# Every matrix product in plain fp32 instead of three split fp32r passes, with the expert weights resident in SBUF

## The reference

```python
# attention, per sequence of n = 256 tokens
xn = layernorm(x) * g_norm
q  = l2norm(xn @ Wq per head) * q_scale              # 16 heads of 64
kv = xn @ Wkv                                        # one key head and one value head of 64
k, v = with a null key and value put in front (one vector, cond_64[0] and cond_64[1])
sim  = 8 * q @ k.T + relative_position_bias          # the bias is a small 3-layer network of i - j
attn = softmax(causal(sim)); out = concat_heads(attn @ v)
x = x + layernorm(out @ Wout) * g_out                # 1024 -> 256
# mixture of experts, per token
scores = softmax((x @ wt.T + cond @ wg.T) / 2)       # 8 experts, the best 2, weights normalised
y_e = (leaky(x @ w_gate[e]) * (x @ w_up[e])) @ w_down[e]      # 256 -> 128 -> 256
x = x + weighted sum of the two y_e + a shared expert of width 256 (as two more blocks of 128)
```

## Time and profile before

| what | us |
|---|---|
| median of three executions (1060.23 to 1061.74) | 1060.24 |
| the profiled execution: its time, its span | 1064.17, 1062.40 |
| to the first transposes of round 0's queries (span's start to 42.89) | 42.89 |
| the rest of round 0, to the transposes of round 1's input | 72.28 |
| rounds 1 to 6, each to the same transposes of the next round | 124.94 to 125.90 |
| round 7 to its output projection | 124.16 |
| output projection of round 7 and its experts | 69.57 |

### The profile page before, as it was taken

One profiled execution on the slowest core, in us unless ns is written; L12 is line 12 of the kernel. 1 busy time (PEld: TensorE's weight loads), 2 busy tenths in 40 slices (PEclk: granted clock), 3 DMA queues, 4 the chain that ended last, 5 costly groups with the idle time before them and its releaser, 6 DMA issues.

```text
span 1062.4 us, 21427 instructions
## 1 busy us (share of the span) xinstructions
PE 1014.6 (96%) x6788; PEld 815.3 (77%) x6788; DVE 707.4 (67%) x2457; ACT 526.5 (50%) x1564; POOL 437.0 (41%) x422
## 2 busy tenths in 40 slices
PE   3887999999999999999999999999999999999998
PEld 2665877778777887778777787777877788777877
DVE  8789577665867558665676647676576755856543
ACT  3488346651565435663456614665246643565220
POOL 1634154441554333642535515454245534444212
PEclk9899999999999999999999999999999999999999
DMA  5316414112132013311132212311123211232043
GB/s 198 80 54 215 151 60 122 53 66 63 61 110 90 28 55 101 100 61 61 43 118 72 71 42 79 112 65 46 62 66 113 82 41 41 84 106 71 20 138 102
DMA packets 40996, 87.68 MB, mean 83 GB/s; under 512 B 4192, under 2 KB 19040, under 8 KB 40624
## 3 DMA queue, kind: packets, MB, share of 16 engines
q1 hardware_dynamic: 39920, 83.57, 24.5%
q10 hardware_dynamic: 960, 2.62, 0.7%
HBM read 76.57 MB, written 9.60 MB: 81 GB/s over the span
## 4 chain that ended last, share of the span: by engine, by line
PE 75%; DVE 10%; issue 5%; ACT 4%; DVEq 0%; POOL 0%; ACTq 0%
PE psY L1641 13%; PE psS L1511 6%; PE psO L1547 5%; PE psG L69 5%; PE psG L71 5%; PE psG L70 5%; PE psT L1522 5%; PE psS L71 3%; PE psS L70 3%; PE psS L69 3%; PE psS L1507 3%; PE psT L1529 2%; PE psO L1550 2%; PE psT L69 2%; PE psT L71 2%
## 5 line engine op out<-in xcount | busy, mean ns | idle before, releaser
L604 POOL TENSOR_TENSOR work<-work,rden 128x514 f32<-128x514 f32 x128 | 134.0, 1047 | 322.3 <-DVE rden L1137 321.6
L1641 PE MATMUL psY<-Wd,H 128*128 128x256 f32 x640 | 172.5, 399 | 0.0
L763 ACT ACTIVATE work<-work,low 128x257 f32<-128x257 f32 x256 | 128.5, 504 | 60.1 <-DVE low L1155 59.5
L69 PE MATMUL psG<-x1T_hi,Wgu 128*128 128x512 f32 (+1 forms) x292 | 134.8, 462 | 2.6 <-ACT leaky L807 1.9
L1641 PEld LDWEIGHTS psY<-Wd,H 128*128 128x128 f32 x640 | 112.4, 190 | 29.4 <-issue 14.4
L1155 DVE CUSTOM_DVE_ANT_0 work<-psS,bias,null_s 128x256 f32<-128x256 f32 x256 | 113.3, 480 | 28.4 <-PE psS L1511 25.9
L1251 DVE SCALAR_TENSOR_TENSOR leaky<-leaky 128x512 f32<-128x512 f32 x80 | 56.4, 704 | 101.5 <-ACT leaky L807 100.5
L71 PE MATMUL psG<-x1T_lo,Wgu 128*128 128x512 f32 (+1 forms) x292 | 114.9, 394 | 0.0
L70 PE MATMUL psG<-x1T_hi,Wgu 128*128 128x512 f32 (+1 forms) x292 | 114.4, 392 | 0.0
L593 POOL TENSOR_TENSOR rq<-qss,neghalf 128x16 f32<-128x16 f32 x32 | 97.5, 3048 | 36.3 <-DVE qss L1131 36.3
L1511 PE MATMUL psS<-KB,qT 64*128 64x256 f32 (+1 forms) x1024 | 105.7, 325 | 0.0
(11 more groups left out here) (259 smaller groups left out, 2306.7 us busy)
## 6 DMA issues: line engine op xcount, KB each, us to landing
Wgu<-wexp SPq DMA_DIRECT2D x80, 512.0 KB, 3.4
Wb<-wscr SPq DMA_DIRECT2D x64, 256.0 KB, 3.6
wexp<-Wgu SPq DMA_DIRECT2D x10, 512.0 KB, 2.9
xres<-in_x SPq DMA_DIRECT2D x8, 512.0 KB, 4.7
xin<-in_x SPq DMA_DIRECT2D x7, 512.0 KB, 4.2
out<-work SPq DMA_DIRECT2D x7, 512.0 KB, 2.9
H<-in_wgu SPq DMA_DIRECT2D x10, 256.0 KB, 3.9
bias<-bscr SPq DMA_DIRECT2D x4, 512.0 KB, 6.6
```

The lines of the kernel that those rows point to most:

```text
L69: te.matmul(dst, a_hi, b_hi, start=start, stop=False)
L604: pool.tensor_tensor(T1[sl][:, hs, :], T1[sl][:, hs, :], rden[sl][:, 1, hs].unsqueeze(2) .to_broadcast([P, 2, N + 1]), ALU.mult)
L763: act.activation(T1[sl][:, h, :], T1[sl][:, h, :], ACT.Exp, scale=-1.0, bias=low[sl][:, 1, h:h + 1], accum_out=den[sl][:, 1, h:h + 1])
L1641: mm = te.matmul(psY[:, t // 2, (t % 2) * D:(t % 2 + 1) * D], H[:, k % H_RING, t * P:(t + 1) * P], Wd[:, ORDER[k], :], start=(k == 0 and t ...
```

## The change

All parts go: every product takes plain fp32 operands and is one `te.matmul` where `products` issued three. `products`, the `lo` tiles, all subtractions and the waits on them are gone; `keys` moves 144 columns instead of 256; head outputs are a ScalarE copy alone; of `xnT` and `x1T` ScalarE copies one half and VectorE the other. The expert weights are loaded once, in round 0, into an SBUF tile that holds all ten blocks, and `wexp`, the ring and the reloads are gone. TensorE waits for all ten loads at the place quoted above.

```diff
-def products(te, dst, a, b, start, stop):
-    (a_hi, a_lo), (b_hi, b_lo) = a, b
-    te.matmul(dst, a_hi, b_hi, start=start, stop=False)
-    te.matmul(dst, a_lo, b_hi, start=False, stop=False)
-    return te.matmul(dst, a_hi, b_lo, start=False, stop=stop)
...
-        Wgu = sb("Wgu", [P, W_RING, 2, 2, KC, P], F32R)
+        Wgu = sb("Wgu", [P, BLOCKS, 2, KC, P])
...
             load_norm_x(1)
-            for e in range(BLOCKS + 2):
-                if e < BLOCKS:
-                    if e >= H_RING:
-                        sp.wait_ge(parts_done.sem, e - H_RING + 1)
-                    sp.dma_start(H[:, e % H_RING, :], wgu[e].rearrange("p w c m -> p (w c m)")) \
-                        .then_inc(wraw_in[e % H_RING].sem, 16)
-                if e >= 2:
-                    sp.wait_ge(parts_done.sem, e - 1)
-                    sp.dma_start(wexp.ap()[e - 2], Wgu[:, (e - 2) % W_RING].bitcast(F32)) \
-                        .then_inc(parts_out[(e - 2) % W_RING].sem, 16)
-            sp.wait_ge(pre_v.sem, V_WOUT)
+            for k in range(BLOCKS):
+                sp.dma_start(Wgu[:, k], wgu[ORDER[k]]).then_inc(ld_gu.sem, 16)
             sp.dma_start(xres[:], x_t[0]).then_inc(xres_in.sem, 16)
...
-                act.activation(oT[0][:, STEPS * (g % 2) + s, (g // 2) * N:(g // 2 + 1) * N], value_bank(n)[:, 0:N],
-                               ACT.Copy).then_inc(o_lead.sem, 1)
+                act.activation(oT[:, STEPS * (g % 2) + s, (g // 2) * N:(g // 2 + 1) * N], value_bank(n)[:, 0:N],
+                               ACT.Copy).then_inc(o_done.sem, 1)
...
-            def head_out(r, n):
-                g, s = n // STEPS, n % STEPS
-                need(dve, o_lead, r, n + 1)
-                cols = (slice(None), STEPS * (g % 2) + s, slice((g // 2) * N, (g // 2 + 1) * N))
-                dve.tensor_tensor(oT[1][cols], value_bank(n)[:, 0:N], oT[0][cols].bitcast(F32), ALU.subtract) \
-                    .then_inc(o_done.sem, 1)
...
+            def x1_turned(m):
+                need(dve, x1T_ps, m, 2)
+                dve.tensor_copy(x1T[:, 1, :], psO[:]).then_inc(x1T_v.sem, 1)
...
-                        mm = products(te, psT[:, t // 2, (t % 2) * 2 * P:(t % 2 + 1) * 2 * P],
-                                      [part[:, c, t * P:(t + 1) * P] for part in xnT],
-                                      [part[:, c, KV0:KV0 + 2 * P] for part in Wall], c == 0, c == KC - 1)
+                        mm = te.matmul(psT[:, t // 2, (t % 2) * 2 * P:(t % 2) * 2 * P + KVN],
+                                       xnT[:, c, t * P:(t + 1) * P], Wall[:, c, KV0:KV0 + KVN],
+                                       start=(c == 0), stop=(c == KC - 1))
...
                 q_half(3, 1).then_inc(q_ps.sem, 1)
                 if moe is None:
                     te.wait_ge(ld_down.sem, 16)
+                if moe is None:
+                    te.wait_ge(ld_gu.sem, 16 * BLOCKS)
                 need(te, kb_a, r, 1)
...
-                        mm = products(te, dst, [part[:, p, t * P:(t + 1) * P] for part in oT],
-                                      [part[:, p, :] for part in Wout], False, p == PAIRS - 1)
+                        mm = te.matmul(dst, oT[:, p, t * P:(t + 1) * P], Wout[:, p, :], start=False, stop=(p == PAIRS - 1))
...
             def gate_up(m, k, w, bank):
                 for c in range(KC):
-                    mm = products(te, bank, [Wgu[:, k % W_RING, part, w, c, :] for part in range(2)],
-                                  [part[:, c, :] for part in x1T], c == 0, c == KC - 1)
+                    mm = te.matmul(bank, Wgu[:, k, w, c, :], x1T[:, c, :], start=(c == 0), stop=(c == KC - 1))
```

More of the change, by code:

```diff
@@ L137, in events @@
             return Events(ctx.enter_context(nc.semaphore(name)), per, base)
-        PARTS = ("hi", "lo")
-        Wall = [sb(f"Wall_{part}", [P, KC, KVN + HEADS * DH], F32R) for part in PARTS]
+        Wall = sb("Wall", [P, KC, KVN + HEADS * DH])
         KV0, Q0 = 0, KVN
-        WtP = sb("WtP", [P, KC, 2 * E], F32R)
-        I2 = sb("I2", [2 * E, E])[:]
-        Wout = [sb(f"Wout_{part}", [P, PAIRS, D], F32R) for part in PARTS]
+        Wout = sb("Wout", [P, PAIRS, D])
         Wd = sb("Wd", [P, BLOCKS, D])
@@ L163, in attention_moe @@
         xres = sb("xres", [P, TILES, D])
-        xnT = [sb(f"xnT_{part}", [P, KC, TOK], F32R) for part in PARTS]
+        xnT = sb("xnT", [P, KC, TOK])
         kvs = sb("kvs", [P, TILES, KVN])
@@ L177, in attention_moe @@
         sq = work[:, 2 * GH * (N + 1):2 * GH * (N + 1) + HEADS * DH]
-        with nc.sbuf_tensor("qT", [P, PAIRS, TOK], F32) as qT:
-            pass
-        oT = [sb(f"oT_{part}", [P, PAIRS, TOK], F32R) for part in PARTS]
+        qT = sb("qT", [P, PAIRS, TOK])
+        oT = qT
         null_s = sb("null_s", [P, TILES, HEADS])
@@ L207, in attention_moe @@
         x1 = sb("x1", [P, TILES, D])
-        x1T = [sb(f"x1T_{part}", [P, KC, TOK], F32R) for part in PARTS]
-        Wgu = sb("Wgu", [P, W_RING, 2, 2, KC, P], F32R)
+        x1T = sb("x1T", [P, KC, TOK])
+        Wgu = sb("Wgu", [P, BLOCKS, 2, KC, P])
         leaky = [sb(f"leaky{i}", [P, TOK]) for i in range(2)]
@@ L287, in logit_bank @@
         def logit_bank(last):
-            return psY[0:2 * E, 1, :] if last else psO[0:2 * E, :]
+            return psY[0:E, 1, :] if last else psO[0:E, :]
         def weight_bank(last):
@@ L330, in attention_moe @@
         bias_in = [events(f"bias_in{i}", 0) for i in range(BIAS_PARTS)]
[L331 to L334, removed]
+        ld_gu = events("ld_gu", 0)
         xin_in = events("xin_in", 16)
@@ L341, in attention_moe @@
         out_in = events("out_in", 16, 16)
-        wgu_ld = [events(f"wgu_ld{i}", 16 * len(range(i, BLOCKS, W_RING))) for i in range(W_RING)]
         ln_var = events("ln_var", 1)
         xn_done = events("xn_done", TILES)
-        xnT_v = events("xnT_v", 3)
+        xnT_v = events("xnT_v", 1)
         mk_done = events("mk_done", 1)
@@ L778, in route @@
             def route(m):
-                for c, bank in ((0, psG), (1, psO)):
-                    need(act, x1T_ps, m, c + 1)
-                    act.activation(x1T[0][:, c, :], bank[:], ACT.Copy).then_inc(x1T_a.sem, 1)
+                need(act, x1T_ps, m, 1)
+                act.activation(x1T[:, 0, :], psG[:], ACT.Copy).then_inc(x1T_a.sem, 1)
             def route_half(m, half):
[L784 to L787, removed]
+                need(act, x1T_ps, m, KC * half + 1)
+                act.activation(x1T[:, 0, half_tokens(half)], psT[:, 0, half_tokens(half)], ACT.Copy) \
+                    .then_inc(x1T_a.sem, 1)
             def logits(m, last=False):
@@ L976, in _, with keys @@
             null_columns()
-            kv_parts()
-            def keys(r, first=False):
+            def keys(r):
                 need(dve, xnT_ps, r, 2)
-                if first:
-                    need(dve, xnT_v, r, 1)
-                else:
-                    dve.tensor_copy(xnT[0][:, 1, :], psT[:, 1, :]).then_inc(xnT_v.sem, 1)
-                for c, ev in ((0, xnT_a), (1, xnT_v)):
-                    need(dve, ev, r, 1)
-                    dve.tensor_tensor(xnT[1][:, c, :], psT[:, c, :], xnT[0][:, c, :].bitcast(F32),
-                                      ALU.subtract).then_inc(xnT_v.sem, 1)
+                dve.tensor_copy(xnT[:, 1, :], psT[:, 1, :]).then_inc(xnT_v.sem, 1)
             def attention(r, moe, following):
@@ L1268, in sums @@
                                   ALU.add).then_inc(ysum.sem, 1)
-            keys(0, True)
-            n = [wall_trail(slice(c, c + 1), 2 * P, Q0 + HEADS * DH) for c in range(KC)]
-            assert n[-1] == V_WALL, n
             positions_second()
@@ L1354, in q_half @@
                 for c in range(KC):
-                    mm = products(te, bank[:, half, :], [part[:, c, t * P:(t + 1) * P] for part in xnT],
-                                  [part[:, c, Q0 + half * 512:Q0 + (half + 1) * 512] for part in Wall],
-                                  c == 0, c == KC - 1)
+                    mm = te.matmul(bank[:, half, :], xnT[:, c, t * P:(t + 1) * P],
+                                   Wall[:, c, Q0 + half * 512:Q0 + (half + 1) * 512], start=(c == 0), stop=(c == KC - 1))
                 return mm
@@ L1565, in turn_half @@
                 if half > 0:
-                    need(te, x1T_v, m, KC * half)
+                    need(te, x1T_a, m, half)
+                    need(te, x1T_v, m, half)
                 for c in range(KC):
@@ L1572, in block_half @@
             def block_half(m, k, w, half):
-                need(te, wgu_ld[k % W_RING], m, 16 * (k // W_RING + 1))
-                need(te, x1T_v, m, KC * (half + 1))
+                need(te, x1T_a, m, half + 1)
+                need(te, x1T_v, m, half + 1)
                 cols = half_tokens(half)
@@ L1578, in block_half @@
                 for c in range(KC):
-                    mm = products(te, bank[:, cols], [Wgu[:, k % W_RING, part, w, c, :] for part in range(2)],
```

(12 more changed lines are left out.)

122 lines of the change are left out of this document (21 added, 101 removed).

## The result

The changed kernel takes 1151.78 us (median of four executions, 1151.03 to 1151.91) where the kernel before takes 1060.24: a ratio of 1.0859, with a 95% interval of 1.084 to 1.0878, 91.5 us slower. The prediction was 1145 us with a range of 1122 to 1160. Its direction, its mechanism and its range hold. It is 6.8 us short: 3.9 us of that are one term of round 0, and 2.7 us lie in two stretches at a lower clock, in the execution that the sum was made against.

A forecast was written before the change was run, and what follows sets the result against it. TensorE was taken to set the pace in rounds 1 to 7 and the last experts; 68.6 us (rounds 1 to 7) + 8.9 (last experts) + 7.0 (round 0) = 84.5, on 1060.24 gives 1145 us, range 1122 to 1160.

The forecast's parts named there:

- The price of a product: On TensorE, a plain fp32 product takes 0.86 us at 512 columns and 0.432 at 256; split, 0.70 and 0.3525.
- The first rival: On TensorE, a plain product of 512 columns takes four fp32r intervals: about +136 us, 1196 us; chance 0.06.
- The round: Rounds 1 to 7: products 11.43 us dearer, less 1.6 us of TensorE's waits: 9.8 us each, 68.6 us in all.
- Round 7 and the last experts: The end of the kernel, from round 7 on: +18.7 us, with +8.9 us of it in the last experts.
- Round 0's wait: TensorE stops for ten expert blocks until about 63, then runs at clock 0.50; VectorE's first score at 70.6, +17.1 us.
- The base: The profiled execution, 1064.17 us, lies 3.93 us above the median, so the sum was added to 1060.24 us.
- Behind that, round 0 gets shorter: Round 0 after VectorE's first score: splits and subtractions go, ScalarE's 2.62 us step remains; 61.65 becomes 51.5 us, 10.1 less.
- four full passes: On TensorE, a plain product of 512 columns costs four fp32r intervals: about +136 us, 1196 us; chance 0.06.
- The dear switch of kinds: On TensorE, changing between fp32 and fp32r costs 71 ns x 288 = 20 us, which goes with the change: 1125 us; chance 0.10.
- The hidden load: In round 0, the expert blocks' load costs nothing net; round 0 is 10 us shorter, not 7 longer: 1128 us; chance 0.08.
- Weight loads: On TensorE, weight loads set the pace; 96 fewer a round take 17.8 us off it: about 918 us; chance 0.02.

The follow-up runs named there:

- The projection alone: The kernel before with only the output projection in plain fp32, head outputs copied once by ScalarE and not subtracted on VectorE: 1077.85 us (1.0166).
- the keys at 256 columns: The changed kernel with its key products moving 256 columns again, still in plain fp32: 1163.31 us.
- the first execution of before: The kernel before, unchanged, in the profiled execution that the prediction made its sum against: 1064.17 us.
- The experiment: The kernel before and the changed kernel, both unchanged, each profiled once more: 1061.27 and 1151.59 us.
- the kernel with the moved wait: The changed kernel with TensorE's wait for the ten expert blocks moved behind round 0, ahead of the first experts: 1132.47 us (1.0678 of before).
- the halved products: The changed kernel with each gate and up product of 512 columns issued as two of 256, doubling matmuls and weight loads: 1152.66 us.

## Why the prediction was right, and where it was short

- **The price of a product** held: 0.858 us for 0.86, 0.431 for 0.432, and the choice of the scaled value over four fp32r intervals was right. Four passes are not refuted by it, only their price: 0.858 is four times 0.2145 us, and it is the fp32r pass that takes longer, 0.2333. By the Trainium skill, "TensorE: Matmul & The Clock Gate", section "Wait — 56ns, not 53.3ns?", a matmul of 512 columns takes 215.7 ns at the full clock; four of these, an estimate, make 0.863 us, so with the four passes of "FP8 and Floating Point Precision", section "TensorE Precision Notes", the trace agrees within 1%. The first rival failed because it priced a pass by fp32r's interval.
- **The round** held: +9.8 predicted, +9.6 measured for each of rounds 1 to 6, with TensorE's 1.6 us of waits filled completely. The projection alone and the keys at 256 columns show two terms of the sum by themselves (2.2 of 2.55 us a round, 11.5 of 11.9 us).
- **Round 7 and the last experts**: +18.7 predicted, +18.5 and +20.2 measured; the spread is the cold stretch behind the router in the first execution of before. So the match with 18.5 is in part luck: it holds 1.7 us that the changed kernel gets back by the clock and that the sum had not counted. At the same clock the sum is 1.5 us short here, and where these are is open.
- **Round 0's wait** held: its end at 63.45 (63), the clock of 0.50 behind it, the first score at 71.11 (70.6). That the end is so near is in part luck: the bias is issued at 45.07, 1.3 us later than before, where the sum had nearly nothing, and the loads queued behind it made most of that up.
- **The base**: 3.93 us were taken off for an execution above the median. The experiment puts 2.7 us of that on two cold stretches, which another execution of before has less of, or not at all. Against that one the change costs 90.5 us, 6.0 more than the sum: 5.5 in round 0 (3.9 in the step that follows, 1.0 in the clock, 0.5 in the first score), -1.0 in the rounds, 1.5 behind them.

**The step that failed** is "Behind that, round 0 gets shorter": 10.1 us were to come back, and 6.2 did (61.65 to 55.49). The loop was sized by ScalarE's 2.62 us a step. In the kernel with the moved wait, whose loop stands behind no stop, VectorE's first scores of the sixteen steps lie 46.4 us apart from first to last (53.88 to 100.27), where the sum had 23.6 + 17.4 + 3 = 44, and the drain behind takes 9.1 where it had 7.5 (its own estimate). By the starts of the scores on TensorE, none of the fifteen distances is under 2.77 us: the nine shortest make 25.4 us where the sum had 23.6, the other six 21.0 where it had 20.4.

With the splits gone the chain goes through TensorE. From the first score to the transposes of round 1 the chain that ended last lists 27.2 us on TensorE, 12.9 on ScalarE and 7.6 on VectorE in the changed kernel; before, it was 15.9, 21.2 and 15.8. In the changed kernel, in order of time (start, us):

```profile
110.70 0.34 PE psS L1372 x2
111.03 0.65 PE psS L1376 x8
111.69 0.58 PE psO L1412 x4
112.27 0.22 PE psO L1415 x4
112.53 0.63 PE psT L1387 x4
113.16 0.22 PE psT L1394 x2
113.47 0.34 PE psS L1372 x2
```

A step is 2.77 us here (110.70 to 113.47): scores, values and transposes, one behind the other on TensorE, which in the whole stretch is busy 49.3 of 55.5 us. An engine relieved hands the pace to the next one, and the sum had not asked which that is. This is read from the chain; no run made TensorE's part of these steps shorter.

Of the rivals, four full passes fall with the 0.429 us. The dear switch of kinds would have given 20 us back with the change; the rounds give back 0.2 us a round more than the terms explain, where 40 products at 71 ns would be 2.8, and the projection alone, which mixes the kinds, came out below its own sum. The hidden load falls with the 18.8 us; its 1128 us are near what the kernel with the moved wait takes. Weight loads fall with the halved products.

## What to carry to other kernels

A list of waits that is nearly empty says that longer work will lengthen the kernel; it doesn't say that shorter work will shorten it as much (9.7 of 17.8 us here): that needs the engine which comes next. Put the wait for a load at its first consumer, not at the last convenient place ahead of it: here that is 17 to 19 of 91 us. And take a change of many parts apart: the one part that shortened the bounding engine's list, the keys, makes the kernel before 0.9% faster alone, while the relief of the others was hidden.

## What was not expected of the hardware

An fp32r pass of 512 columns takes 0.2333 us, 9% more than a quarter of a plain fp32 product (0.2145), so three split passes cost 0.82 of the plain product and not 0.75. And the granted clock behind the same short stop differs between executions of one kernel: behind the 1.91 us for the router it averaged 0.69 once and 1.00 once over 1019.5 to 1025, while behind the stop of 19 us it was at the lower level in both executions of the changed kernel.
